# Column maxima of the last two attention chunks on GpSimd instead of by TensorE turns

## The reference

```
x_norm = (x - mu) / sqrt(var + EPS) * gamma + beta
q, k, v = x_norm @ qkv            # 512 x 512 each
scores = where(causal, q k^T / sqrt(512), -inf)
attn = softmax(scores, axis=-1)
out = (attn @ v) @ o_proj + residual
h = silu(x @ w_gate) * (x @ w_up);  keep the 2 largest of each 4;  ffn = h_sparse @ w_down
```

## Time and profile before

| | |
|---|---|
| median of three runs | 793.25 us (792.91, 793.25, 793.26) |
| profiled execution, first to last instruction (its span) | 791.1 us |
| what lies around the span, median less span | 2.15 us |
| mean granted TensorE clock | 1.000 |
| busy in the span: PE, DVE, ACT, POOL | 787.2, 606.0, 316.9, 10.7 us |

### The profile page before, as it was taken

How to read it: one execution, slowest core, us unless ns; L and a number is a source line. 1 busy time by engine, 2 the same in 40 slices (tenths; PEclk the granted TensorE clock), 3 DMA queues, 4 the chain that set the end, 5 groups by cost and what they waited for, 6 DMA issues and landing times.

```text
span 791.1 us, 9390 instructions
## 1 busy us (share of the span) xinstructions
PE 787.2 (100%) x3560; PEld 653.1 (83%) x3560; DVE 606.0 (77%) x979; ACT 316.9 (40%) x514; POOL 10.7 (1%) x23
## 2 busy tenths in 40 slices
PE   9999999999999999999999999999999999999998
PEld 6888888888888888888888888888888888888887
DVE  6978787477644797789989789798658658559786
ACT  5423222235122464464634634363424334335431
POOL 2010101000000000000000000000000000000000
PEclk9999999999999999999999999999999999999999
DMA  9541462300131524586454452697277163161002
GB/s 321 184 161 64 136 241 89 112 28 0 54 94 41 211 119 175 170 310 240 186 174 173 186 165 128 245 351 288 100 259 269 57 239 117 70 240 53 1 1 106
DMA packets 31612, 121.75 MB, mean 154 GB/s; under 512 B 3088, under 2 KB 3664, under 8 KB 29136
## 3 DMA queue, kind: packets, MB, share of 16 engines
q1 hardware_dynamic: 29120, 116.90, 40.2%
q10 hardware_dynamic: 2448, 4.26, 1.7%
HBM read 77.07 MB, written 44.07 MB: 153 GB/s over the span
## 4 chain that ended last, share of the span: by engine, by line
PE 99%; DMA 1%; SPq 0%; DVE 0%; issue 0%
PE bank L969 13%; PE bank L971 13%; PE bank L970 13%; PE bank L689 10%; PE bank L687 10%; PE bank L688 10%; PE bank L840 8%; PE bank L1049 7%; PE bank L1051 7%; PE bank L1050 7%; DMA raw<-L_attn_qkv 1%; PE bank L762 0%; PE bank L795 0%; PE bank L697 0%; PE bank L1062 0%; PE bank L1061 0%
## 5 line engine op out<-in xcount | busy, mean ns | idle before, releaser
L969 PE MATMUL bank<-X_hi,wset 128*128 128x512 f32 x448 | 174.6, 390 | 0.0
L971 PE MATMUL bank<-X_hi,wset 128*128 128x512 f32 x448 | 174.5, 389 | 0.0
L970 PE MATMUL bank<-X_lo,wset 128*128 128x512 f32 x448 | 174.5, 389 | 0.0
L971 PEld LDWEIGHTS bank<-X_hi,wset 128*128 128x128 f32 x448 | 84.1, 188 | 17.5
L969 PEld LDWEIGHTS bank<-X_hi,wset 128*128 128x128 f32 x448 | 84.1, 188 | 17.4 <-issue 0.2
L970 PEld LDWEIGHTS bank<-X_lo,wset 128*128 128x128 f32 x448 | 84.1, 188 | 17.3
L1049 PE MATMUL bank<-dw,hs_hi 128*128 128x512 f32 x224 | 87.4, 390 | 0.0
L1051 PE MATMUL bank<-dw,hs_lo 128*128 128x512 f32 x224 | 87.3, 390 | 0.0
L1050 PE MATMUL bank<-dw,hs_hi 128*128 128x512 f32 x224 | 87.2, 389 | 0.0
L1694 DVE TENSOR_TENSOR acc<-bank,acc 128x512 f32<-128x512 f32 x59 | 40.2, 688 | 40.1 <-PE bank L1051 39.6
L1049 PEld LDWEIGHTS bank<-dw,hs_hi 128*128 128x128 f32 x224 | 42.1, 188 | 8.9 <-DVE acc L1694 0.2
(11 more groups left out here) (263 smaller groups left out, 1491.0 us busy)
## 6 DMA issues: line engine op xcount, KB each, us to landing
w_operands<-wset SPq DMA_DIRECT2D x8, 3584.0 KB, 14.0
wset<-w_operands SPq DMA_DIRECT2D x8, 3584.0 KB, 11.4
wsum<-w_units SPq DMA_DIRECT2D x28, 256.0 KB, 3.6
dw_raw<-L_ffn_w_down SPq DMA_DIRECT2D x14, 512.0 KB, 5.0
xw<-L_attn_x SPq DMA_DIRECT2D x4, 1024.0 KB, 9.6
xt_raw<-x_t SPq DMA_DIRECT2D x8, 512.0 KB, 7.5
xn_t<-xt_raw SPq DMA_DIRECT2D x8, 512.0 KB, 2.8
acc<-resid SPq DMA_DIRECT2D x2, 2048.0 KB, 10.2
```

What stands on the lines that cost most here:

```text
L969: pe.matmul(dst[:], u[:, 0, :], x_hi, start=(first and kt == 0), stop=False, skip_group_check=True)
L970: pe.matmul(dst[:], u[:, 0, :], x_lo, start=False, stop=False, skip_group_check=True)
L971: last = pe.matmul(dst[:], u[:, 1, :], x_hi, start=False, stop=(kt == 1), skip_group_check=True)
```

## The change

The transposes, the two DVE steps and the ACT copy go. POOL makes `max_all` out of `max_one` with one `partition_all_reduce` for each chunk, as soon as `max_fold` is done. `max_all` of chunk 2 moves from 140 to 92 KB. The first meeting of a chunk takes over the waits for the banks 4 to 7 that `turn_max` held, and SP waits for the second reduction before it loads B22, whose place covers `max_one` of chunk 3.

```diff
+MAX = bass.bass_isa.ReduceOp.max
...
-              xh_pre[3][3], xh[3][2], *u[10:], ("max_fold", 2, 0), xh[3][3], *z_round[3][0:2], ("max_turn", 2, 0), *z_round[3][2:4], ("max_spread", 2, 0),
-              *z[3][0:2], ("max_keep", 2, 0)]
+              xh_pre[3][3], xh[3][2], *u[10:], ("max_fold", 2, 0), ("max_all", 2, 0), xh[3][3], *z_round[3], *z[3][0:2]]
...
-              ("X_load", 0, 0), ("max_turn", 3, 0), v[3][0], v_keep[0], ("max_spread", 3, 0), *v[3][1:4], ("max_keep", 3, 0)]
+              ("max_all", 3, 0), ("X_load", 0, 0), v[3][0], v_keep[0], *v[3][1:4]]
...
-                             for name, o, shape in (("sum_pair", (136, 168), [P, 2, W]), ("max_all", (140, 172), [P, W])))
+                             for name, o, shape in (("sum_pair", (136, 168), [P, 2, W]), ("max_all", (92, 172), [P, W])))
...
                     load_T(T1)
+                    sp.wait_ge(max_reduced, len(WIDE))
                     load_X(X_raw[B22], X_loaded[B22], 2, 1)
...
+                elif kind == "max_all":
+                    pool.wait_ge(max_folded, n - WIDE[0] + 1)
+                    nc.gpsimd.partition_all_reduce(out_ap=max_all[n][:], in_ap=max_one[n][:], channels=P, reduce_op=MAX).then_inc(max_reduced, 1)
...
-            def turn_max(c):
-
-                pe.wait_ge(rows_ready, TC * c)
-                pe.wait_ge(turn_free, len(turn_no))
-                pe.wait_ge(max_folded, c - WIDE[0] + 1)
-                turn_four(bank[4], lambda b: max_one[c][:, b * P:(b + 1) * P], max_turned)
-
-            def spread_max(c):
-                pe.wait_ge(max_rows_ready, c - WIDE[0] + 1)
-                turn_four(bank[5], lambda b: max_rows[c][:, b, :], max_spread)
...
             def meet_values(c, j):
 
+                if j == 0:
+                    pe.wait_ge(rows_ready, TC * c)
+                    pe.wait_ge(turn_free, len(turn_no))
                 pe.wait_ge(wide_ready, parts_ahead[c] + j + 1)
...
                         pe.wait_ge(wide_kept, N_UNITS - PROD_RING + 1 + k)
-
-                        if k == 1:
-                            turn_max(n)
-                            product(kind, n, k, (xT_hi[n], xT_lo[n]), k * P, (vo_hi, vo_lo), 3, spread_max)
-                            continue
...
-                elif kind == "max_keep":
-                    act.wait_ge(max_spread, n - WIDE[0] + 1)
...
-                    nc.scalar.copy(max_all[n][:], bank[5][:]).then_inc(max_kept, 1)
...
                 if j == 0:
-                    dve.wait_ge(max_kept, c - WIDE[0] + 1)
+                    dve.wait_ge(max_reduced, c - WIDE[0] + 1)
...
-                elif kind == "max_turn":
-                    dve.wait_ge(max_turned, n - WIDE[0] + 1)
-                    done = step(nc.vector.reduce_max(wide_max[:], bank[4][:].rearrange("p (b k) -> p b k", k=P), AX.X))
-                    dve.wait_ge(vec_step, done)
-                    nc.vector.tensor_scalar(max_rows[n][:], wide_max[:].rearrange("p (b o) -> p b o", o=1).broadcast_to((P, TC, P)), 1.0, None,
-                                            ALU.mult).then_inc(max_rows_ready, 1)
```

More of the change, by code:

```diff
@@ L239, in attention_ffn @@
         wide_hi = {c: at(f"wide_hi{c}", o * KB, [P, 2, 2 * W], F32R) for c, o in ((2, 128), (3, 160))}
-        max_pair, max_one, max_rows = ({c: at(f"{name}{c}", o[c - 2] * KB, shape, F32) for c in WIDE}
-                                       for name, o, shape in (("max_pair", (112, 16), [P, 2, W]), ("max_one", (118, 20), [P, W]),
-                                                              ("max_rows", (116, 22), [P, TC, P])))
+        max_pair, max_one = ({c: at(f"{name}{c}", o[c - 2] * KB, shape, F32) for c in WIDE}
+                             for name, o, shape in (("max_pair", (112, 16), [P, 2, W]), ("max_one", (118, 20), [P, W])))
         sum_pair, max_all = ({c: at(f"{name}{c}", o[c - 2] * KB, shape, F32) for c in WIDE}
-                             for name, o, shape in (("sum_pair", (136, 168), [P, 2, W]), ("max_all", (140, 172), [P, W])))
+                             for name, o, shape in (("sum_pair", (136, 168), [P, 2, W]), ("max_all", (92, 172), [P, W])))
         rows_late = at("rows_late", 156 * KB, [P, 2, W], F32)
@@ L294, in attention_ffn @@
         ident, causal, causal_t = small("ident", [P]), small("causal", [P]), small("causal_t", [P])
-        wide_max = small("wide_max", [TC])
         gamma_t, beta_t = small("gamma_t", [KT]), small("beta_t", [KT])
@@ L336, in attention_ffn @@
         wide_full, wide_kept, max_folded = sem("wide_full"), sem("wide_kept"), sem("max_folded")
-        max_turned, max_rows_ready, max_spread, max_kept = sem("max_turned"), sem("max_rows_ready"), sem("max_spread"), sem("max_kept")
+        max_reduced = sem("max_reduced")
         shifted, exp_made, wide_hi_ready, wide_ready = sem("shifted"), sem("exp_made"), sem("wide_hi_ready"), sem("wide_ready")
@@ L709, in cols, with product @@
                 return t[0][:, k, a:b], t[1][:, k, a:b]
-            def product(kind, n, k, lhs, a, rhs, amid=0, other=None):
+            def product(kind, n, k, lhs, a, rhs):
                 pairs, dst = [(cols(lhs, q, a, a + P), cols(rhs, q, 0, W)) for q in range(KT)], bank_of_product(prod_no[kind, n, k])[:]
[L713 to L716, removed]
+                three(dst, pairs).then_inc(prod_full, 1)
             def keys_of(t, count, q):
@@ L948, in _ @@
                     wide_scores(n, k)
[L949 to L952, removed]
                 elif kind == "meet":
@@ L1213, in _ @@
                         nc.scalar.copy(raw_unit(n, k), prod_bank[k % PROD_RING][:, 0:W - unit_cols(n, k)]).then_inc(wide_kept, 1)
-                elif kind == "max_keep":
-                    act.wait_ge(max_spread, n - WIDE[0] + 1)
-                    if n == WIDE[0]:
-                        act.wait_ge(prod_full, prod_no["z", NCH - 1, KT - 1] + 1)
-                    nc.scalar.copy(max_all[n][:], bank[5][:]).then_inc(max_kept, 1)
                 elif kind == "exp_wide":
```

## The result

| | |
|---|---|
| median of the kernel with the change | 799.35 us (798.67 to 799.92, 4 runs) |
| median of the kernel before, same chip | 793.25 us (792.91 to 793.86) |
| ratio | 1.0075, 95% interval 1.0061 to 1.0089 |
| profiled execution | 798.67 us, span 796.9 us, mean granted clock 0.996 |

A forecast was written before the change was run, and what follows sets the result against it. PE's own chain was taken to bound the kernel. Turns saved and waits in chunks 3 and 2 summed as -1.92 + 4.77 + 0.14 = +3.0 us, from 793.25 to 796.2 us; range 791.2 to 812.

The forecast's parts named there:

- Two turns of chunk 3 cost 0.97, the pair of chunk 2 0.95: Transposes of the maximum on PE in chunks 2 and 3: removing them takes 1.92 us off the chain.
- D = 8.0 us: Duration of one POOL reduction, priced as 8 passes: seven halvings of the partitions and one pass to write the result.
- The lower bound of one pass: POOL's reduction cannot be shorter than one pass over 512 elements per partition, 1.0 us at the select's rate.
- a D outside 6.7 to 16: Sign that the prediction is wrong: a POOL reduction lasting less than 6.7 or more than 16 us.
- S = D + 0.1: Time from the fold's end to the first shift: the reduction's duration plus two handovers, 8.1 us.
- S - 3.33: PE's wait in chunk 3, up to the third meeting: fold-to-shift time less 3.33 us, 4.77 us in the sum.
- S - 7.96: PE's wait in chunk 2, tightest at the fourth meeting: fold-to-shift time less 7.96 us, 0.14 us in the sum.
- the bank from S = 8.8: Chunk 2's third value product: its bank holds PE only once fold-to-shift time reaches 8.8 us, as part of the same wait.
- The instruction without operands ahead of the first reduction has 34 us: On POOL, free from 136.45: this instruction has 34 us before chunk 2's fold ends at 170.69, so costs nothing.
- The first call is dear: Rival: POOL's first reduction costs 6 us more, chunk 2 waits 6.1 us, the time is 802.2 us; chance 0.06.
- What costs nothing: Reductions run while DVE is mostly idle or reads banks; SP's later B22 load and the first meeting's bank waits cost nothing.
- the rival of 0.25: The reduction is short, under 3.5 us: PE hardly waits, the turns are saved, 791.3 us; chance 0.25.

The follow-up runs named there:

- the two versions free of the start's loss: The changed kernel with PE's constants wait moved to its first transposes, 791.27 us; the changed kernel with a small POOL add behind the second reduction, 791.21 us.
- the last experiment: The changed kernel, with PE's constants wait moved to its first transposes, and chunk 2's reduction done seven times: 798.06 us, ratio 1.0062.

## Why the prediction was right and wrong

The direction, and the range of 791.2 to 812, held, and both by luck. The forecast of 796.2 us came 3.2 us short, by a mechanism that did not happen; without the part that it missed the kernel would have come out at 791.3, its low end.

- **"Two turns of chunk 3 cost 0.97, the pair of chunk 2 0.95"**: right. The four products take 10.90 us, the folds and the end move by 0.96 and 1.1 us, and the two versions free of the start's loss gain 1.85 and 1.91 us against 1.92.
- **"D = 8.0 us"**: wrong by a factor of four, and the reason that the forecast's wait never came. A reduction of 128 x 512 took 2.19 the first time and 1.78 us from then on, 1.88 (chunk 3, four in a row) to 1.95 us (chunk 2, seven in a row, the longer first one among them) from start to start with the waits between. In passes of the select at 1.0 us for 512 that is about two, where I had counted eight: seven halvings with a pass each was the wrong picture of the work. The lower bound of one pass was nearer than either value inside, and a D outside 6.7 to 16 is one of the prediction's own signs of being wrong. The figure of the Trainium skill, GPSIMD Engine Reference (Cross-partition — where GPSIMD wins), from which I estimated 62 us, is for another instruction and not borne out for this one: the measurement decides.
- **S = D + 0.1**: right in kind. From fold to reduction it is 0.10 us in chunk 3 and 0.13 to 0.14 in chunk 2, from reduction to shift, where the shift waits for it, 0.04; in sum D + 0.14 to D + 0.18.
- **S - 3.33 in chunk 3**: right, 4.22 against 4.28 measured. **S - 7.96 in chunk 2, and the bank from S = 8.8**: right for the bank, 4.84 against 5.05; 5.68 against 6.8 for the whole, since the clock's 1.68 us come on top of the bank's wait where PE idles for 4.9 us.
- **"The instruction without operands ahead of the first reduction has 34 us"**: true, and the step that failed. I asked whether its own place covers it and stopped there. The same instruction stands ahead of POOL's first select, and what the added one leaves behind decides what that one costs. Two things were to be seen: the program's order, where the row stands in both kernels, and the chain of waits at the start, where PE waits for POOL's constants with some 2 us to spare (the second select ended at 2.03 us, PE's last warming matmul began at 4.14). An event that costs 9.6 us needs only to land in front of that.
- **"The first call is dear"**, chance 0.06: the right kind of cost and nearly its size, at the wrong place. I priced 6 us on the first reduction. There it was hidden, as the text said; at the start of the next execution it was not.
- **"What costs nothing"** for the load of B22 and the banks of the first meeting: right.

The chance of slower, 0.5, came true by a case to which the prediction gave no place at all; on what it did know, the reduction's duration, its likeliest value lost to the rival of 0.25.

## What to carry to other kernels

Let an engine wait for constants at the step that reads them and not at its front: that costs nothing here (793.31 against 793.12 us), and how late the constants come matters less.

Both ways made the same gain out of the change: 791.21 and 791.27 us, 0.23 to 0.24% under the kernel before and 8.1 us under the change as it was made. Either would do; the two together were not tried.

## What the runs showed of the hardware

- What an execution leaves on POOL holds into the next. Without a change of library the idle time ahead of the first select is a few tenths (0.24 us before, 0.49 with library 0 asked for again at the end); with one it takes 9.6 to 10.1 us at the start, 8.3 us at 260 us and 6.0 us at 145 us, none of it with a row of its own. The DMA engines' share in these three stretches was 0.90 to 0.93, 0.48 and 0.37, which goes in the same order; that their traffic lengthens the load was not tested.
- `partition_all_reduce` with a maximum over 128 partitions: 0.39 us for 4 columns of fp32, 1.78 us for 512, 2.19 us for the first of an execution.
- The granted clock fell to 0.50 after PE had been idle from 4.4 us, and in the last experiment to 0.61 in the mean behind 4.9 us without a matmul; the gap itself and the slower matmuls behind it add up.
